# One adaLN transformer block on one core: other engine orders, modulation taken as columns, four input tiles normalised by GpSimd

## What is computed

```python
def _L0_attn_ref(x, wq, wk, wv, wo):      # 32 heads of 128, 8 key/value heads, T = 1024, D = 512
    q, k = q * cos + _rotate_half(q) * sin, k * cos + _rotate_half(k) * sin
    scores = jnp.einsum('bhtd,bhsd->bhts', q, k) * (1.0 / np.sqrt(HD))
    att = jax.nn.softmax(jnp.where(mask, scores, -jnp.inf), axis=-1)
    return jnp.einsum('bhts,bhsd->bhtd', att, v).transpose(0, 2, 1, 3).reshape(B, T, H * HD) @ wo
...
mod = (_silu(L0_c) @ L0_wmod).reshape(L0_c.shape[0], 6, 1, -1)
sa, ca, ga, sb, cb, gb = (mod[:, 0], mod[:, 1], mod[:, 2], mod[:, 3], mod[:, 4], mod[:, 5])
ga = (2 * (ga >= 0) - 1) * jnp.maximum(jnp.abs(ga), 0.25)
gb = (2 * (gb >= 0) - 1) * jnp.maximum(jnp.abs(gb), 0.25)
h = _layernorm(x, axis=-1) * (1 + ca) + sa
x = x + ga * _L0_attn_ref(h, L0_attn_wq, L0_attn_wk, L0_attn_wv, L0_attn_wo)
h = _layernorm(x, axis=-1) * (1 + cb) + sb
x = x + gb * _L0_ffn_ref(h, ...)          # dense 512 x 512, plus a low-rank part with a router
```

## Time and profile before

| | |
|---|---|
| median of 3 runs | 1097.12 us (1095.56 to 1098.68) |
| the profiled execution | 1097.11 us, span 1095.3 us |
| mean granted TensorE clock | 0.991 of full |
| busy in the span | TensorE 1053.4 us (96%), VectorE 773.5 (71%), ScalarE 634.4 (58%), GpSimd 520.0 (47%) |
| DMA | 86.92 MB, mean 79 GB/s |

### The profile page before, as it was taken

One profiled execution on the slowest core, in us unless ns is written; L12 is line 12 of the kernel. 1 busy time (PEld: TensorE's weight loads), 2 busy tenths in 40 slices (PEclk: granted clock), 3 DMA queues, 4 the chain that ended last, 5 costly groups with the idle time before them and its releaser, 6 DMA issues.

```text
span 1095.3 us, 16543 instructions
## 1 busy us (share of the span) xinstructions
PE 1053.4 (96%) x5426; PEld 872.2 (80%) x5426; DVE 773.5 (71%) x1831; ACT 634.4 (58%) x1301; POOL 520.0 (47%) x506
## 2 busy tenths in 40 slices
PE   6999999999999999999999999999999999999997
PEld 3668878888888878887888878888787878888775
DVE  4668866688558866688657865689657875688576
ACT  5547764477437754477436754477436763577433
POOL 2535653365425653365434643455524652455244
PEclk8999999999999999999999999999999999999999
DMA  6462233132302233132312223023212224022001
GB/s 214 149 218 76 87 97 78 36 100 87 94 13 68 87 97 78 35 101 87 82 25 68 78 84 99 11 94 109 58 58 68 78 78 106 6 96 73 21 20 59
DMA packets 98285, 86.92 MB, mean 79 GB/s; under 512 B 39380, under 2 KB 84052, under 8 KB 98072
## 3 DMA queue, kind: packets, MB, share of 16 engines
q1 hardware_dynamic: 98200, 85.86, 26.4%
HBM read 59.23 MB, written 26.61 MB: 78 GB/s over the span
## 4 chain that ended last, share of the span: by engine, by line
PE 58%; DVE 12%; ACT 9%; DMA 8%; POOL 5%; issue 5%; SPq 2%; POOLq 0%; DVEq 0%; ACTq 0%
PE accumulators L705 16%; PE accumulators L675 14%; PE accumulators L690 11%; PE scores L625 9%; DMA pa_lo<-p_rows 4%; PE transposed L638 4%; DMA p_rows<-turned 3%; DVE p_large L1213 3%; ACT p_large L929 3%; DVE turned L1239 2%; PE scores L894 2%; DVE o_lo L1258 2%; POOL qc L1601 2%; DVE pb_lo L1225 1%; POOL qr L1597 1%
## 5 line engine op out<-in xcount | busy, mean ns | idle before, releaser
L1588 POOL TENSOR_SCALAR p_large<-p_large,rowinv 128x640 f32<-128x640 f32 (+3 forms) x128 | 125.3, 979 | 234.8 <-DVE rowinv L1218 234.8
L937 ACT ACTIVATE pb_hi<-transposed 128x512 fp32r<-128x512 f32 (+3 forms) x256 | 118.1, 509 | 178.6 <-PE transposed L638 178.4
L1597 POOL TENSOR_TENSOR qr<-qr,trig 128x512 f32<-128x512 f32 x80 | 106.2, 1327 | 206.8 <-ACT qr L962 206.8
L929 ACT ACTIVATE p_large<-p_large,negmax 128x640 f32<-128x640 f32 (+3 forms) x128 | 126.4, 988 | 99.3 <-DVE negmax L1213 98.2
L1225 DVE TENSOR_TENSOR pb_lo<-transposed,pb_hi 128x512 fp32r<-128x512 f32 (+3 forms) x256 | 141.8, 585 | 58.7 <-ACT pb_hi L937 58.3
L1213 DVE CUSTOM_DVE_ANT_0 p_large<-scores,mask 128x640 f32<-128x640 f32 (+3 forms) x128 | 130.0, 1016 | 18.4 <-PE scores L625 14.9
L625 PE MATMUL scores<-k_hi,q_hi 128*128 128x512 f32 (+2 forms) x384 | 139.5, 363 | 1.7 <-DVE negmax L1213 1.7
L625 PE MATMUL scores<-k_hi,q_lo 128*128 128x512 f32 (+2 forms) x384 | 131.7, 343 | 0.0
L1588 POOL TENSOR_SCALAR p_small<-p_small,rowinv 128x128 f32<-128x128 f32 (+3 forms) x128 | 97.2, 774 | 71.6 <-DVE rowinv L1218 71.6
L625 PE MATMUL scores<-k_lo,q_hi 128*128 128x512 f32 (+2 forms) x384 | 131.0, 341 | 0.0
L1601 POOL TENSOR_TENSOR qc<-qc,qr 128x512 f32<-128x512 f32 x80 | 116.6, 1458 | 6.5 <-POOL qr L1597 0.3
(11 more groups left out here) (169 smaller groups left out, 2224.4 us busy)
## 6 DMA issues: line engine op xcount, KB each, us to landing
p_rows<-turned SPq DMA_DIRECT2D x31, 640.0 KB, 2.9
pa_lo<-p_rows SPq DMA_DIRECT2D x124, 160.0 KB, 3.2
stage<-in_L_attn_wq_dram SPq DMA_DIRECT2D x32, 256.0 KB, 2.8
stage<-in_L_attn_wo_dram SPq DMA_DIRECT2D x32, 256.0 KB, 3.4
v_rows<-vt SPq DMA_DIRECT2D x32, 128.0 KB, 2.8
v_lo<-v_rows SPq DMA_DIRECT2D x32, 128.0 KB, 3.2
y<-in_L_wmod_dram SPq DMA_DIRECT2D x4, 512.0 KB, 5.6
stage<-in_L_attn_wk_dram SPq DMA_DIRECT2D x8, 256.0 KB, 2.7
```

The costliest lines, as they stand in the source:

```text
L929: nc.scalar.activation(row(i), row(i), ACT.Exp, bias=negmax[:, i:i + 1], scale=-1.0, accum_out=rowsum[:, i:i + 1]).then_inc(s_exp, 1)
L937: nc.scalar.activation(pt_of(i, part, True), src, ACT.Copy).then_inc(t_hi, 1)
L1588: nc.gpsimd.tensor_scalar(row(i), row(i), rowinv[:, i:i + 1], 1.0, ALU.mult, ALU.mult).then_inc(s_norm, 1)
L1597: nc.gpsimd.tensor_tensor(qr[:, s, :], qr[:, s, :], trig[:, 1, half * HALF:(half + 1) * HALF], ALU.mult).then_inc(r_sin, 1)
```

## The change

It does five things.

1. **Modulation as columns.** `first` (`sa` and `ca`) and `second` (`sb` and `cb`) are now 32 float32 matmuls each, with a 128 x 128 block of `mod_w` as weights and one column of `silu` moving. The row copies and the turning of rows into columns go. `second` stands at place 3 of head 0 alone. DVE takes `first` right behind the statistics of tile 4. SyncE's transfer for `ga` waits for `second`.
2. **Input tiles 4 to 7** are normalised by GpSimd (`xn_late`), each behind its own root and shift.
3. **First weights** are split one step sooner, at n = 3, 4 (ACT) and 2, 3 (DVE).
4. **GpSimd's rotary step of the next head** is cut: sine product, normalise tile 6, sum, normalise tile 7.
5. **Orders of ACT and DVE.** In the heads 1 and 2 `early_hi` and `early_lo` go ahead of the split of the rotated `q`; in the last head they go behind the exponential of tile 7 and the swap (cosine) of `k0`.

```diff
@@ fillers
-        (0, 2): wo(0) + mod("sb"),
-        (0, 3): wo(1) + mod("cb"),
-        (0, 4): wo(2, 3) + mod("second") + [("q", (1, 0), 0)],
+        (0, 2): wo(0),
+        (0, 3): wo(1) + mod("second"),
+        (0, 4): wo(2, 3) + [("q", (1, 0), 0)],
@@ sync
-            sp.wait_ge(a_full, N.value("a", ("mod", "sb"), g0))
+            sp.wait_ge(a_full, N.value("a", ("mod", "second"), g0))
             sp.dma_start(mod_w[:, :, 0:D], wmod_v[:, :, 2 * D:3 * D]).then_inc(mod_in[1], 16)
-            sp.wait_ge(a_full, N.value("a", ("mod", "cb"), g0))
@@ tensor, modulation
-                    pe.wait_ge(a_taken, N.value("a", name, at) - 1)
-                    for n in range(2 * KC):
-                        mm = nc.tensor.matmul(acc[:, n:n + 1], vt[0:1, n * P:(n + 1) * P], ident[0:1, 0:1],
-                                              start=True, stop=True)
+                    for k in range(KC):
+                        if m == "first":
+                            pe.wait_ge(mod_in[k], 16)
+                        elif k == 0:
+                            pe.wait_ge(mod_in[0], 32)
+                        for n in range(2 * KC):
+                            mm = nc.tensor.matmul(acc[:, n:n + 1], mod_w[:, k, n * P:(n + 1) * P], silu[:, 3, k:k + 1],
+                                                  start=(k == 0 and n == 0), stop=(k == KC - 1 and n == 2 * KC - 1))
@@ tensor, start
-                        pe.wait_ge(xn_done, 4 * (half + 1))
+                        pe.wait_ge((xn_done, xn_late)[half], 4)
@@ scalar, back
+                if h in (1, 2):
+                    early_hi(h, at)
                 rotated_hi(("q", ((h + 1) % R, 0)), at, int(last))
                 if last:
                     split_hi(("v", 0), at, 1)
-                if h:
-                    early_hi(h, at)
...
                 exp(h, 7, at)
-                if not h:
+                fill(h, 5, at, slice(0, 1) if last else slice(0, -1))
+                if h in (0, 3):
                     early_hi(h, at)
-                fill(h, 5, at, slice(0, -1))
+                if last:
+                    fill(h, 5, at, slice(1, -1))
@@ vector, start
                 norm(x_tile(t), t, ln_var)
+                if t == KC:
+                    take_modulation("first", Group(0))
@@ gpsimd, back
-                rotate(("q", ((h + 1) % R, 0)), at, int(last))
+                rotate_sin(("q", ((h + 1) % R, 0)), at, int(last))
                 normalise(h, 6, at)
+                rotate_sum(("q", ((h + 1) % R, 0)), at, int(last))
                 normalise(h, 7, at)
@@ gpsimd, start
                 root_and_shift(t, ln_var, ln_stat)
+                if t >= 4:
+                    pool.wait_ge(ln_stat, t + 1)
+                    nc.gpsimd.tensor_scalar(x_tile(t), x_tile(t), rstd[:, t:t + 1], shift[:, t:t + 1], ALU.mult,
+                                            ALU.add).then_inc(xn_late, 1)
```

67 lines of the change are left out of this document (28 added, 39 removed).

## The result

The changed kernel takes 1111.22 us (median of 5 executions, 1106.66 to 1112.93) where the kernel before took 1097.12. The ratio is 1.0119, with a 95% interval of 1.0091 to 1.0147: slower by some 13 us. The profiled execution is the one of 1111.22 us, its span 1109.4 us, 14.1 longer than before.

The account below looks back on a forecast made before the run. It took TensorE as the bound, busy 1053.4 of 1095.3 us, its waits small and repeated. Start +1.0, second modulation -0.7, last heads +1.9, third heads +2.6, second head +0.2 gave +5.0, 1102.1 us; 8 in 10 range 1093 to 1108.

Parts of the forecast that it names:

- Start, +1.0 forecast: Input stage: `first` done at 18.5, tile 7 at 24.9, swap of `k0` at 31.3 against 30.33, +1.0 us.
- half-clock loads at twice the price: Rival: weight loads cost 0.234 at half clock; start +3.8, second modulation +0.6, orders +4.7, total 1106.2 us; chance 0.15.
- Second modulation, -0.7 forecast: TensorE around `second`: scores 5, 64 records, projection and the clock's way back take 14.8 us instead of 15.5.
- upper bound of +0.6: Second modulation's worst case: records priced at 0.234 at half clock, +0.6 us.
- `ga` and `gb`, nothing forecast: Transfers issued from about 60 us against 59.8 before: no cost.
- The condition that I did name (TensorE 4 us sooner): Second modulation: the `ga` and `gb` transfers cost nothing unless TensorE arrives 4 us sooner.
- Last heads, +1.9: Last head of a group, seven times: `q` 1.82 us later, less 1.17 and `pa_hi`'s wait w; +1.9 us.
- third heads, +2.6 forecast: Third head, eight times: exponential and so tile 7 later, about 0.33 us each after slack; +2.6 us.
- First heads, nothing forecast: First head of a group: output products cover everything, no cost.
- Second head, +0.2 forecast: Second head: a shift of 0.6 us meets a slack of about 0.6; +0.2 us in all.
- the orders do what they move: Rival: `q` is not held up, seven waits of 10.5 us vanish; -10.2, 1086.9 us; chance 0.12.

Follow-up runs that it names:

- second_only: The kernel before with the second modulation as columns alone; 1101.71 us, ratio 1.0041.
- late_take: The changed kernel with VectorE's take-up of `first` behind all eight statistics instead of behind the fifth; 1111.87 us, 1.0111 of the kernel before.
- columns_wide: The changed kernel with 64 equal columns moved behind each weight block in both modulations instead of one; 1108.08 us, 1.0082 of the kernel before.
- head3_wide: head3_only with the second modulation as 64 weight blocks and 64 equal columns behind each; 1086.75 us, 0.9889 of the kernel before.
- start_only: The kernel before with the input stage alone: `first` as columns, GpSimd normalising tiles 4 to 7, weights split one step sooner; 1104.85 us, 1.0056.
- rotation_whole: The changed kernel with GpSimd's rotation whole again, sine product and sum ahead of tile 6; 1090.52 us, 0.9942 of the kernel before.
- head3_only: The kernel before with `pa_hi` and `pa_lo` moved behind the swap and cosine product of `k0` in the last heads alone; 1084.97 us, 0.9883.
- cut_only: The kernel before with GpSimd's rotation cut alone (sine product, tile 6, sum), `pa_hi` and `pa_lo` where they were; 1137.31 us, 1.0348.
- gpsimd_only: The kernel before with tiles 4 to 7 normalised by GpSimd and weights split one step sooner, both modulations as rows; 1100.93 us, 1.0022.
- first_columns: The kernel before with the first modulation as columns alone, ScalarE normalising all tiles; 1101.11 us, 1.0021.
- orders_only: The kernel before with the cut rotation and the conversions `pa_hi` and `pa_lo` moved in heads 1 to 3; 1105.9 us, 1.0070.

## Why the prediction was wrong

The direction was right, the size was not: +5.0 us forecast, 1102.1 us, range up to 1108; measured +13 to +14. The step that failed outright is the one on the first heads; the start and the second modulation were mis-sized. Step by step:

**Start, +1.0 forecast, +3.6 measured.** The mechanism was right in each link: the one-column products did not raise the clock, tile 5's statistics wait for `first`, GpSimd's tiles follow one another at 1.75 us (1.7 forecast, its product 0.77 for the 0.75 taken). What was mis-sized is the record price at half clock: 0.214 us (13.68 / 64), not the 0.19 taken. I had set it by four weight loads at half clock; twice the full-clock price, 0.234, was nearer. It moves `first` by 1.3 us; tile 7 came at 26.5 (24.9 forecast). The rest: TensorE took up the second half with its clock still half, and the way from there to the swap was 7.3 us (26.57 to 33.91) and not the 6.4 of the forecast (0.7 + 5.7). The rival "half-clock loads at twice the price" had +3.8 for this stage, near the +3.6, but in part by luck: it had `first` at 21.3 and tile 7 at 27.7, both over 1 us too late, and the longer way to the swap made up for it. The forecast looked for a clock of 0.50 in the windows from 10 to 18 us. They read 1.00: the profile has no record of the clock ahead of its first change. The durations say half: two transposes take 0.43 us from start to start at 20.19 to 20.62, against 0.22 at full clock in the kernel before:

```profile
16.40 0.38 PE L787 MATMUL scores<-ident,qr 128*128 128x128 f32 x2
16.62 0.38 PE L787 MATMUL scores<-ident,qc 128*128 128x128 f32 x2
```

The Trainium skill (TensorE: Matmul & The Clock Gate, What's actually happening) says that the throttled state is the default from which activity releases the clock; the durations agree with that default, the clock column does not show it.

**Second modulation, -0.7 forecast, +1.8 measured (+5.2 in `second_only`, 20.7 us for 15.5 between the same two points).** "The clock is full when they begin and will fall while they run; where is chance" was right for the changed kernel, where it fell within the records and without an idle time; in `second_only` and `late_take` it was half before they began. Two terms were mis-sized. The split into 44 records at full clock and 20 at half was about 32 and 32 in the changed kernel (3.4 us of full clock, the other 7.0 us at half), 10.4 us instead of 8.9; in `second_only` it was none and 64. And the clock was half already under the scores ahead (tile 5's took 2.56 us, 52.56 to 55.12, instead of 1.3). The projection with the clock's way back, 4.6 forecast, took 4.35. So the upper bound of +0.6 was none: it allowed a half clock only from within the records on. (By the forecast's own terms, 44 records at 0.117 and 20 at 0.234, it would be +0.2.) TensorE waits 1.7 us for `negmax` right ahead of scores 4, and behind that wait the clock fell in six of the fourteen traces; a bound has to take the clock as half for the whole stretch.

**`ga` and `gb`, nothing forecast, 0.95 us measured.** I looked at SyncE's transfers and not at VectorE, where `ga` stands behind `q_lo`, which the cut delays. The condition that I did name (TensorE 4 us sooner) is exactly what `columns_wide` and `head3_wide` ran into.

**Last heads, +1.9, and third heads, +2.6 forecast; together +3.9 measured** between third and last head. `q_hi` is 1.8 us later against the sine product, as the sum said: it starts 3.2 us behind the end of that product (772.89 + 1.30, 777.39), and before it was 1.4 us (764.13 in the earlier trace rows) behind the end of this row:

```profile
761.43 1.30 POOL L1597 TENSOR_TENSOR qr<-qr,trig 128x512 f32<-128x512 f32 x1 [0.66 <-ACT qr L962]
```

TensorE's wait grew from 1.10 to 1.70 where w, the time for which `pa_hi` waited for its transfer, is 0 (+0.60, forecast +0.65). The total is 11.9 us in seven waits (12.7 forecast); before it was 10.8 in eight, of which one, 0.4, is not in a last head. The transposes' wait for `p_large` is there, but it grew from 1.6 us in 8 to 2.9 in 8, 0.16 each and not 0.33. The mechanism of this part, the largest of the forecast, held: each link is in the rows. That its total came so near (3.9 for 4.5) is in part luck, since the w of the forecast was read from one trace, and it differs between executions (`start_only`, with the same orders, has 3.1 us more in this stretch). That the cut and not the move is the loss is shown: `rotation_whole`, which differs by the cut alone, is some 20 us faster than the changed kernel, `head3_only` wins 12.9 us and `cut_only` loses 38.

**First heads, nothing forecast, +3.6 measured.** This is the step that failed: "In the first head output products cover everything", a term put at nothing. They cover ScalarE and GpSimd. They don't cover VectorE, since they themselves wait for VectorE's additions, and these are queued behind `q_lo`. Followed along VectorE's queue, the 1.8 us of the cut would have been seen there. `rotation_whole` shows the cause: 43.77 again; and `cut_only` has 44.3 in this row with nothing but the cut.

**Second head, +0.2 forecast, -0.8 measured** for the two middle stretches, no error that matters.

In short: the trace is 9.1 us over the forecast (14.1 - 5.0). 3.6 of these are the first heads, 2.6 the start, 2.5 the second modulation, 0.95 `ga` and 0.7 the first group, less 0.6 in the last and third heads and 1.0 in the second; that makes 8.8. Half of it is one queue (VectorE behind `q_lo`), the rest is mostly work at half clock, in and around the one-column products. The rival on the other side, "the orders do what they move", named the right lever: `q_hi` not held up, seven waits gone. It takes the rotation whole.

**What stays open.** Why at the start 64 columns per block did not bring the clock up either (64 records in 13.7 us, 0.214 each, in `columns_wide`), while the row products of the kernel before did within their first half. Why the clock falls behind some waits and not behind others of the same length. And why `start_only`, `gpsimd_only` and `first_columns` are slower in their medians than their starts account for. In `start_only` and `first_columns` the clock is not the reason: their mean clocks, 0.991 to 0.994 and 0.989 to 0.996, are no lower than those of the kernel before beside them (0.988 to 0.994 and 0.986 to 0.994). Their traces show 3.1 and 2.0 us more in front of the last heads, which may be part of it; no trace of a slower execution was taken.

## What to carry to other kernels

When an instruction is delayed, follow every queue in which something waits for it, and not only the chain for which the move was made: here the conversion was paid for on ScalarE, and the additions behind it on VectorE cost as much again. Take such a change apart before judging it: the moves of the conversions and the cut, which belong together on paper, were worth -7.8 and +38 us alone and +7.7 together. And where a reordering takes out a wait, look at how that wait varies from group to group before you count it. In this kernel the records with one moving column had to be priced at half clock from the first one, and the work behind them too. Last, look at which transfer is next late before counting what a faster form would give.

## What the runs showed of the hardware

- A float32 product of a 128 x 128 block costs, per record (two records a product), 0.211 to 0.214 us at half clock and 0.110 to 0.112 at full clock, with one column (changed kernel, `second_only`) and with 64 (`columns_wide`) alike: up to 64 columns the number of columns did not change the price. With weights of one row, in L719 before, it was 0.117 at full clock.
- While one-column records ran, the clock was half throughout in two places (13.8 us of them at the start of the changed kernel, 13.5 in `second_only`), and in the changed kernel it fell 3.4 us into an unbroken run of them. Under 64 columns it stayed full for 7 us at the second modulation (`columns_wide`, `head3_wide`) and half for 13.7 us at the start (`columns_wide`). Under the 512-column row products of `orders_only` it went from half to full.
- TensorE's waits of 2.8 us in the last heads were followed by 3.4 us of half clock in six of seven groups (`cut_only`), and each time three products of four matmuls took 1.6 us more. Behind a wait of 2.23 us in the kernel before the clock stayed full, behind one of 1.94 it fell.
- GpSimd's one-input product over 128 x 512 with two factors per partition takes 0.76 to 0.77 us, also with VectorE at work beside it.
